# Mixture-of-experts stage of a four-stage kernel: an expert's 192 slots as 128 + 64 rows instead of 96 + 96

## The reference, cut to what matters

```python
_, topk_idx = jax.lax.top_k(scores + bias[None, :], K)      # K = 6 of E = 32
...
valid = pos < CAP                                           # CAP = 192
xb = jnp.zeros((E, CAP + 1, Hd), x.dtype).at[eid, pos].set(h_rep)
g = jnp.einsum('ech,eih->eci', xb, w_gate)                  # 512 -> 256
u = jnp.einsum('ech,eih->eci', xb, w_up)
inter = jax.nn.silu(g) * u
yb = jnp.einsum('eci,ehi->ech', inter, w_down)              # 256 -> 512
y = yb[eid, pos] * w_slot[:, None]
routed = y.reshape(-1, K, Hd).sum(axis=1)
```

## Time and profile before

| | |
|---|---|
| runs | 1627.20, 1628.32, 1631.93 us; median 1628.32 |
| the profiled execution: span from first to last instruction | 1626.5 us; 1.8 us below the median of the runs (no other time is given for it) |
| busy share | PE 87%, DVE 69%, ACT 39%, POOL 27% |
| granted clock of PE, mean | 0.962 |
| first to last expert, `up(0)` to the last `down` | from 1295.5 to 1608.3 us |

### The profile page before, as it was taken

How to read it: one execution, slowest core, us unless ns; L and a number is a source line. 1 busy time by engine, 2 the same in 40 slices (tenths; PEclk the granted TensorE clock), 3 DMA queues, 4 the chain that set the end, 5 groups by cost and what they waited for, 6 DMA issues and landing times. The chain is left out here.

```text
span 1626.5 us, 27691 instructions
## 1 busy us (share of the span) xinstructions
PE 1415.8 (87%) x8733; PEld 836.7 (51%) x8733; DVE 1121.3 (69%) x2715; ACT 641.7 (39%) x1452; POOL 439.7 (27%) x382
## 2 busy tenths in 40 slices
PE   2588888888888879999988999999689899999995
PEld 1244454444444444444445555565334477777773
DVE  6899999999999954554654677787765644444310
ACT  4344344434434452333225667666430022222221
POOL 3243444334443410000011000000010255555552
PEclk8699999999999979999999999999799999999998
DMA  8432323222323030000000000000231378888884
GB/s 275 68 98 82 87 72 102 77 78 76 100 77 83 9 117 0 0 0 0 1 27 13 14 25 15 13 0 1 85 138 46 107 204 239 233 242 245 244 246 92
DMA packets 75895, 147.71 MB, mean 91 GB/s; under 512 B 14244, under 2 KB 43908, under 8 KB 71600
## 3 DMA queue, kind: packets, MB, share of 16 engines
q1 hardware_dynamic: 61920, 112.85, 22.1%
q0 software_dynamic: 13904, 33.97, 8.9%
HBM read 112.29 MB, written 34.48 MB: 90 GB/s over the span
## 5 line engine op out<-in xcount | busy, mean ns | idle before, releaser
L357 ACT ACTIVATE probs_t<-ps_sc 128x512 f32<-128x512 f32 x256 | 152.9, 598 | 305.8 <-PE ps_sc L455 305.8
L771 DVE TENSOR_SCALAR nf_above<-nf_scaled 128x512 f16<-128x512 bf16 x495 | 201.6, 446 | 0.0
L1048 PE MATMUL f_ps<-f_xt,w_t 128*128 (+1 forms) x704 | 158.5, 379 | 4.9 <-DVE f_xt L993 2.5
L671 DVE TENSOR_REDUCE row_max<-ps_max 128x2 f32<-128x384 f32 (+1 forms) x256 | 157.1, 615 | 7.7 <-PE ps_max L438 7.4
L2436 DVE TENSOR_TENSOR d_inter<-d_silu_g,d_su 128x384 f32<-128x384 f32 x32 | 17.7, 554 | 189.8 <-PE d_su L2181 182.8
L435 PE MATMUL ps_max<-band_mask,identb 128*128 128x384 bf16 (+1 forms) x256 | 94.3, 368 | 52.0 <-DVE row_max L671 32.3
L314 POOL TENSOR_TENSOR nf_above<-nf_above 128x1536 f16<-128x1536 f16 x33 | 102.4, 3102 | 129.8 <-DVE nf_above L771 129.8
L501 PE MATMUL ps_nf<-nf_above,ident_f 128*128 128x512 f16 x264 | 94.9, 388 | 23.2 <-DVE nf_w L781 21.2
L2193 PE MATMUL d_sy<-d_wdown,d_inter 128*96 128x512 f32 x256 | 115.0, 592 | 0.0
L1048 PEld LDWEIGHTS f_ps<-f_xt,w_t 128*128 128x128 bf16 x704 | 68.8, 98 | 87.5 <-issue 4.5
L1631 ACT ACTIVATE c_probs<-c_s,c_negmax 128x128 f32<-128x128 f32 x256 | 90.6, 366 | 56.8 <-DVE c_negmax L1716 56.0
(11 more groups left out here) (314 smaller groups left out, 2797.6 us busy)
## 6 DMA issues: line engine op xcount, KB each, us to landing
d_wgu<-in_ex_gu SPq DMA_DIRECT2D x32, 1024.0 KB
d_wdown<-in_ex_d SPq DMA_DIRECT2D x32, 512.0 KB
dr_parts<-qk_parts SPq DMA_DIRECT2D x16, 768.0 KB, 4.5
q_stack<-dr_parts SPq DMA_DIRECT2D x192, 64.0 KB, 2.8
k_stack<-dr_parts SPq DMA_DIRECT2D x192, 64.0 KB, 2.9
out<-x_sb SPq DMA_DIRECT2D x17, 256.0 KB
nf_w<-in_nf_w POOLq DMA_DIRECT2D x3, 1408.0 KB, 14.7
x_sb<-in_x SPq DMA_DIRECT2D x4, 1024.0 KB, 6.9
```

The lines of the kernel that those rows point to most:

```text
L357: act.activation(pt[:, c, :], SP[c % 2][:].rearrange("p a w -> p (a w)"), ACT.Exp, scale=D0 ** -0.5).then_inc(s_e, 1)
L671: dve.tensor_reduce(mx[:, g, 8 * hp + qt:8 * hp + qt + QT + 1:QT], M[c % 2][:, :, off:off + hi - lo], AX.X, ALU.max).then_inc(s_mx, 1)
L771: op = dve.tensor_scalar(above[:, g, k, :], lvl[:, g, :], STEPS[k], LEVELS[k + 1] - LEVELS[k], ALU.is_gt, ALU.mult)
L1048: mm = pe.matmul(bank[:], w12[:, m, kt, ft * P:(ft + 1) * P], xt[:, q, kt, bass.ds(g * N, N)], start=(kt == 0 and q == 0), stop=(kt == KT ...
```

## The change

The slots are cut at 128 and not at 96. The first part (`a == 0`) has 128 slots, the second 64.

- `turn`: for each `t` a transpose of 128 x 128 and one of 64 x 128 (into 64 columns), alternating. The first takes the tile 128 x 128, the second 64 x 128.
- `down`: the first part streams 512 columns as before, now with 128 weight columns. The second has 64 weight columns, a tile of 128 x 64. It is issued twice for each `it`, for output columns 0 to 255 in the array's left half and 256 to 511 in the right half, into partitions 0 to 63 and 64 to 127 of the same 256 columns of the bank.
- `weigh`: one eviction of 128 x 512 and two of 64 x 256.
- `lists_turn`: one transpose of 128 x 128, and the last 64 slots twice by a float32 matmul with the identity, so that their weights stand on partitions 64 to 127 too.
- Gathers and scatters have 128 and 64 rows. The small list tiles have 128 partitions.

```diff
-    HC = CAP // 2
+    S0 = P
+    S1 = CAP - P
...
-    xg = h[0:HC, 0:8, :].rearrange("p (b a) d -> p b a d", a=2)
-    yo = h[0:HC, 8:12, :].rearrange("p (b a) d -> p b a d", a=2)
+    xg = [h[:, 0:4, :], h[0:S1, 4:8, :]]
+    yo = [h[:, 8:10, :], h[0:S1, 10:12, :]]
...
-    YP = [b[0:HC, :] for b in YB]
+    H2 = D // 2
+    rows_of = [slice(0, S0), slice(0, S1)]
...
             def lists_turn(q):
                 pe.wait_ge(s_lc, q + 1)
                 ge(pe, s_lr, q)
-                for a in range(2):
-                    mm = pe.transpose(LTB[:, a, :], lsb[:, a * HC:(a + 1) * HC], ident[:])
+                pe.transpose(LTB[:, 0, :], lsb[:, 0:S0], ident[:])
+                for k in range(2):
+                    mm = pe.matmul(LTB[S1 * k:S1 * k + S1, 1, :], lsb[:, S0:CAP], ident[:], start=True, stop=True, skip_group_check=True)
                 mm.then_inc(s_ltn, 1)
...
                 for t in range(KT):
-                    for a in range(2):
-                        mm = pe.transpose(XB[t // 2][:, t % 2, a * HC:(a + 1) * HC], xg[:, buf, a, t * P:(t + 1) * P], ident[0:HC, 0:HC])
+                    pe.transpose(XB[t // 2][:, t % 2, 0:S0], xg[0][:, buf, t * P:(t + 1) * P], ident[:])
+                    mm = pe.transpose(XB[t // 2][:, t % 2, S0:CAP], xg[1][:, buf, t * P:(t + 1) * P], ident[0:S1, 0:S1])
                 mm.then_inc(s_xt, 1)
...
                     for it in range(IT):
-                        mm = pe.matmul(YP[a], it_[:, par, it, a * HC:(a + 1) * HC], wd[:, par, it, :], start=(it == 0), stop=(it == IT - 1))
+                        if a == 0:
+                            mm = pe.matmul(YB[0][:], it_[:, par, it, 0:S0], wd[:, par, it, :], start=(it == 0), stop=(it == IT - 1))
+                        else:
+                            for k in range(2):
+                                mm = pe.matmul(YB[1][S1 * k:S1 * k + S1, 0:H2], it_[:, par, it, S0:CAP], wd[:, par, it, k * H2:(k + 1) * H2],
+                                               start=(it == 0), stop=(it == IT - 1), skip_group_check=True)
                     mm.then_inc(s_dn, 1)
...
-                    act.activation(yo[:, par, a, :], YP[a], ACT.Copy,
-                                   scale=gw[:, bass.ds(e, 1), a:a + 1].rearrange("p o a -> p (o a)")).then_inc(s_yo, 1)
+                    weight = gw[:, bass.ds(e, 1), a:a + 1].rearrange("p o a -> p (o a)")
+                    if a == 0:
+                        op = act.activation(yo[0][:, par, :], YB[0][:], ACT.Copy, scale=weight)
+                    else:
+                        for k in range(2):
+                            part = slice(S1 * k, S1 * k + S1)
+                            op = act.activation(yo[1][:, par, k * H2:(k + 1) * H2], YB[1][part, 0:H2], ACT.Copy, scale=weight[part])
+                    op.then_inc(s_yo, 1)
```

More of the change, by code:

```diff
@@ L1831, in phase_layer1_moe @@
     wd = sb("d_wdown", [P, 2, IT, D], F32)
-    gidx = sb("d_gather_at", [HC, NE, 2], U32)
-    sidx = sb("d_scatter_at", [HC, NE, 2], U32)
-    gw = sb("d_slot_w", [HC, NE, 2], F32)
+    gidx = sb("d_gather_at", [P, NE, 2], U32)
+    sidx = sb("d_scatter_at", [P, NE, 2], U32)
+    gw = sb("d_slot_w", [P, NE, 2], F32)
     h_dram = nc.dram_tensor("dr_h", [NB * P, D], F32).ap()
@@ L1938, in phase_layer1_moe @@
     oneb = sb("d_ones", [P, P], BF16)
-    dump = sb("d_dump_row", [HC, 2], F32)
+    dump = sb("d_dump_row", [P, 2], F32)
     tmp = [sb(f"d_tmp{k}", [P, NB, NE], F32) for k in range(3)]
@@ L1953, in phase_layer1_moe @@
     lsb = sb("d_list_rows", [P, CAP], F32)
-    lists = sb("d_lists", [HC, 2, 4, NV], F32)
-    tok = sb("d_list_token", [HC, 2, 4], F32)
-    lw = sb("d_list_tmp", [HC, 2, 4], F32)
+    lists = sb("d_lists", [P, 2, 4, NV], F32)
+    tok = sb("d_list_token", [P, 2, 4], F32)
+    lw = sb("d_list_tmp", [P, 2, 4], F32)
     si = sb("d_shared_in", [P, 2, IT, GT], F32)
-    xg = h[0:HC, 0:8, :].rearrange("p (b a) d -> p b a d", a=2)
-    yo = h[0:HC, 8:12, :].rearrange("p (b a) d -> p b a d", a=2)
+    xg = [h[:, 0:4, :], h[0:S1, 4:8, :]]
+    yo = [h[:, 8:10, :], h[0:S1, 10:12, :]]
     xt = h[:, 12:15, :].rearrange("p r d -> p (r d)").rearrange("p (b k c) -> p b k c", b=2, k=KT)
@@ L1963, in phase_layer1_moe @@
     it_ = sb("d_inter", [P, 2, IT, CAP], F32)
-    gst = sb("d_gather_now", [HC, 4, 2], U32)
-    sst = sb("d_scatter_now", [HC, 2, 2], U32)
+    gst = sb("d_gather_now", [P, 4, 2], U32)
+    sst = sb("d_scatter_now", [P, 2, 2], U32)
     GB = [ctx.enter_context(nc.psum_tensor(f"d_sg{k}", [P, GT], F32)) for k in range(2)]
@@ L1970, in phase_layer1_moe @@
     LB = ctx.enter_context(nc.psum_tensor("d_lb", [P, NB * NE], F32))
-    LTB = ctx.enter_context(nc.psum_tensor("d_ltb", [P, 512], F32))[0:HC, 0:2 * P].rearrange("p (a c) -> p a c", a=2)
+    LTB = ctx.enter_context(nc.psum_tensor("d_ltb", [P, 512], F32))[:, 0:2 * P].rearrange("p (a c) -> p a c", a=2)
     slots = lambda b: b[:, 0:2 * CAP].rearrange("p (i c) -> p i c", c=CAP)
     XB, GP, UP = [slots(b) for b in GB], slots(UB[0]), slots(UB[1])
-    YP = [b[0:HC, :] for b in YB]
+    H2 = D // 2
+    rows_of = [slice(0, S0), slice(0, S1)]
     s_k, s_ch, s_act, s_pos = sem("d_const"), sem("d_route_step"), sem("d_route_act"), sem("d_pos_mm")
@@ L2011, in _ @@
             pool.iota(iof[:], [[1, CAP]], base=0, channel_multiplier=0, allow_small_or_imprecise_dtypes=True).then_inc(s_k, 1)
-            pool.iota(dump[:], [[HC, 2]], base=NB * P, channel_multiplier=1, allow_small_or_imprecise_dtypes=True).then_inc(s_k, 1)
+            pool.iota(dump[:], [[S0, 2]], base=NB * P, channel_multiplier=1, allow_small_or_imprecise_dtypes=True).then_inc(s_k, 1)
             pool.memset(oneb[:], 1.0).then_inc(s_k, 1)
@@ L2041, in gather @@
                 for a in range(2):
-                    pool.indirect_dma_start(xg[:, buf, a, :], None, h_dram,
-                                            bass.IndirectOffsetOnAxis(ap=gst[:, buf, a:a + 1], axis=0)).then_inc(s_gt[buf], 16)
+                    pool.indirect_dma_start(xg[a][:, buf, :], None, h_dram,
+                                            bass.IndirectOffsetOnAxis(ap=gst[rows_of[a], buf, a:a + 1], axis=0)).then_inc(s_gt[buf], 16)
             def scatter(e, par, start):
@@ L2053, in scatter @@
                 for a in range(2):
-                    pool.indirect_dma_start(out, bass.IndirectOffsetOnAxis(ap=sst[:, par, a:a + 1], axis=0),
-                                            yo[:, par, a, :], None, compute_op=ALU.add).then_inc(s_sc, 16)
+                    pool.indirect_dma_start(out, bass.IndirectOffsetOnAxis(ap=sst[rows_of[a], par, a:a + 1], axis=0),
+                                            yo[a][:, par, :], None, compute_op=ALU.add).then_inc(s_sc, 16)
             quad_vals(0)
@@ L2348, in list_done @@
                 step(dve.tensor_scalar(lw[:], lists[:, :, :, 5], -1.0, 1.0, ALU.mult, ALU.add))
-                step(dve.tensor_tensor(lw[:], lw[:], dump[:].rearrange("p (a o) -> p a o", o=1).broadcast_to((HC, 2, 4)), ALU.mult))
+                step(dve.tensor_tensor(lw[:], lw[:], dump[:].rearrange("p (a o) -> p a o", o=1).broadcast_to((P, 2, 4)), ALU.mult))
                 step(dve.tensor_tensor(tok[:], tok[:], lw[:], ALU.add))
```

## The result

The changed kernel is slower, by about what was forecast: 1655.18 us (median of 4 runs, 1652.63 to 1656.00) against 1630.12 for the kernel before in the same comparison (4 runs, 1627.20 to 1632.28), a ratio of 1.0158 with a 95% interval of [1.0140, 1.0175]. The forecast was 1656 us, in a range of 1638 to 1671. The profiled execution took 1656.0 us with a span of 1654.4 us, against 1626.5 before. So the loss is 25.1 us by the medians and 27.9 us, the very figure of the forecast, by the two profiled executions.

A forecast was written before the change was run, and what follows sets the result against it. PE was taken to set the pace, the DMA not far behind. Terms +40.6 (`turn`) - 13.8 (`down`) - 2.4 + 3.6 (lists) - 0.4 (waits) + 0.3 (tail) = +27.9 us on 1628.3 gave 1656 us, range 1638 to 1671.

The forecast's parts named there:

- The waits for `d_wgu`: PE's waits for these weights, read as 1.0 us in all, mostly go with a longer expert: -0.4 us.
- `turn`, +1.27 us: Seven changes between row tiles inside `turn` and one on leaving for `down`: +1.27 us per expert, x 32 = +40.6 us.
- The step from one row with two columns: For `turn`: row-tile changes cost the same 0.095 us as column-tile ones, inferred from one place with two-column matmuls.
- The prediction's step to 0.109 us: In `turn`, a 128-column transpose lasts 29 ns longer than a 96-column one of 0.082 us, so 0.109 us.
- Rival 1: Row tiles in `turn` are free, it stays at 0.66 us, and the kernel gets faster: 1616 us; chance 0.12.
- rival 2: The array drains, but weights for `turn`'s transposes load while it empties: 13 to 16 us go, 1641 us; chance 0.08.
- rival 3: Emptying the array after a transpose in `turn` takes the whole 0.166 us: +18 us, 1674 us; chance 0.07.
- `down`, -0.444 us: Second half of `down` as two side-by-side column groups, 1.272 us for 1.716: -0.444 us, x 31 = -13.8 us.
- rival 4: The two column halves of `down` don't run at once: +0.81 x 31 = +25 us, 1681 us; chance 0.05.
- the lag of the second column group: In `down`'s second half, the second group starts about one weight load late: 0.058 us.
- The 79% of ideal: Skill's packing figure for three column tiles; for `down`'s two groups 1.09 us and not 0.92, sum 5 us higher.
- `lists_half` and `lists_turn`: `down` needs no exit before `lists_half`, 12 x -0.202 = -2.4 us; `lists_turn` takes 0.69 for 0.22, +3.6 us in all.

The follow-up runs named there:

- e1: Changed kernel with `turn`'s four 128-row transposes issued first, then its four 64-row ones, 2 changes of tile for 8: 1628.32 us, 0.9996 of the kernel before.
- e4: Changed kernel with `turn`'s transposes issued as 128, 64, 64, 128 rows and so on, 4 changes of tile for 8: 1637.88 us, 1.0057 of the kernel before.
- e2: Changed kernel with the 64 slots turned with 96 rows, so no change of tile in `turn`: 1623.59 us, 0.9967 of the kernel before.
- e6: e2 with the second part of `down` issuing all left-half matmuls first, then the right half's: 1620.04 us, 0.9946 of the kernel before.
- e2b: e2 run again unchanged, in the second group of runs: 1620.71 us, 0.9949 of the kernel before.
- e5: e2 with the list turn's two 64-column matmuls issued before its transpose: 1618.46 us, 0.9933 of the kernel before.
- e7: No changes of tile in `turn`, as in e2, and the second part of `down` in one piece of 512 columns: 1636.50 us, 1.0045 of the kernel before.
- e3: Changed kernel with the second part of `down` in one piece, 512 columns on the whole array: 1674.29 us, 1.0274 of the kernel before.

## Why the prediction was right

**What bounds the kernel.** PE before and after, with no wait that took its place; each us per expert on PE came out at the end. The waits for `d_wgu` went with the longer expert, as said; they were less than the prediction read, since its row of 1.0 us is that of the weight loads, and PE's own wait was 0.2 us.

**`turn`, +1.27 us.** Measured 1.88 - 0.66 = +1.22. The step from one row with two columns to eight transposes of 64 to 128 columns held: seven changes of 0.15 and an exit of 0.19 (put at 0.153 and 0.202). The prediction's step to 0.109 us for a 128-column transpose, 0.082 + 0.029, gives 0.111, but the chain has 0.11 and 4 x 0.109 in e1. Rival 1 needed a cost below 0.40 us; rival 2 needed the weights hidden, and they load in the open; rival 3 needed 0.07 us more per change. The Trainium skill (TensorEngine Tiling (Array Packing), Key Properties) says that a change of tiling mode drains the engine, and its modes include tiles of 64 rows; the trace agrees. e1, e4 and e2 give it a price: 0.14 to 0.16 us on average with the first weights.

**`down`, -0.444 us.** Measured 1.21 - 1.72 = -0.51. The halves run at once (rival 4 falls). The mis-sized term is the lag of the second column group: put at 0.058 us, one weight load, and measured at 0.007. The two groups load their weights side by side too. The trace of the kernel before had a hint of this: the router's four tiles start within 0.020 us of each other (1183.443 to 1183.463 us), though from the second wave on three of them stand 0.03 behind the first. The 79% of ideal that the prediction weighed from the Trainium skill (TensorE: Matmul & The Clock Gate, Measured speedup vs the span model), a figure for three tiles, would make it 1.09 us behind the first weights; the trace of these two tiles has 0.864 + 0.007 = 0.87 and doesn't agree.

**`lists_half` and `lists_turn`.** The gate behind `lists_half` takes 2.80 us in both kernels, and in the changed one every gate does: the 0.202 that the sum took off is there. `lists_turn` takes 0.26 + 0.37 for 0.22, so +0.41 and not +0.47: the lag of 0.058 that isn't there, again. The four distances from one `up` to the next in a quad went from 9.30, 10.15, 10.29 and 9.59 to 10.02, 10.78, 10.81 and 10.62: +2.90 in all (one by one they don't compare well, since a start holds part of the exit before it), against 4 x 0.71 - 2 x 0.20 + 0.41 = 2.85 from the pieces.

**The sum.** By the terms of the sum a quad was to grow by 4 x 0.83 - 0.40 + 0.47 = 3.39 us; it grew by 2.90. Five lags (0.25) and four times the 0.05 of `turn` (0.20) are most of the difference. Over the whole span (us; the sum's terms are dealt out to the parts by how often each occurs there, of the seven list turns six behind `up(2)`):

| part | by the sum's terms | measured |
|---|---|---|
| `up(2)` to `up(31)` | 23.9 | 20.35 |
| this stage up to `up(0)`, then to `up(2)` without the dip, tail | 4.0 | 2.4 |
| dip of the clock at `up(1)` | none | 3.0 |
| before this stage, where neither program differs | none | 2.2 |
| all | 27.9 | 27.9 |

So the terms came to 22.7 us and not 27.9, and two things that are not in the sum filled up the rest. The range had room for one such dip, and the place where it would come was not foreseen. That the span is 1654.4 on both sides is therefore partly luck; each of the two large terms was right to within 0.07 us per expert.

## What to carry to other kernels

- Count the changes of tile shape in a row of small matmuls before you cut its operands: here each cost some 0.15 us, as much as the stream of 180 float32 transpose columns, and it shows as no idle time. Order the instructions by tile, not by loop index: e1 gets back all that the change had cost that way, with not one instruction more or less.
- A short operand that would take a smaller tile can be padded up to one that takes the whole array (96 rows for 64 in e2). Four times 0.03 us of streaming bought back eight changes.
- Column halves that stream different columns can be worth it where a matmul has 64 weight columns and is long enough: here they saved 0.51 us of 1.72 with both changes paid. Shorter ones and fewer columns were not tried.

## What was not expected of the hardware

- The second column group starts 0.007 us (0.013 in e6) behind the first, with its own weight load beside it, and the groups take their matmuls past each other in the program (e6).
- The dip of the granted clock behind `up(0)`. In the changed kernel it is at 0.50 for 6.8 us from 1306.5 us, after the stretch in which PE was busy half the time. e4 has one too, in the same place and half as long (a stretch of it):

```profile
1305.60:1309.00 3.40, 3.40 (x14) 3.04 (x14) 1.45 (x9) 0.00 (x0) 0.00 (x0) 0.50 0.25 104
```

So do e2, e2b, e5, e6 and e7 (3.4 us each) and e3 (6.8 us); e1 has one of 6.8 us earlier, at 1276.6. The kernel before waited for the same list rows there for 1.8 us and had none. What decides whether and how long was not tested; it is open. The dips differ from kernel to kernel, so a us or two of the differences between medians may be theirs and not the edits'.
- In e1, e2 and e4 the chain has pauses of 0.03 to 0.35 us in the middle of a gate at the start of a turn of the loop, put down to "issue", where neither data nor weights were late:

```profile
1516.31 1.66 PE d_su L2181 x9
1517.97 0.19 issue
1518.16 1.39 PE d_su L2181 x7
```

Five experts of e2 take 10.14 to 10.29 us where the same program in its second profile, e2b, takes 9.71 to 9.80, 2.3 us in all; the view of waits gives PE 1.0 us of such pauses. The kernel before and the changed one have none of them. Why PE's next instructions come late there was not tried, and stays open.
